# Third attention of a four-layer block: second mask by ScalarE, context projections moved, masks loaded in two steps

## What is computed

```
q = _w8a8_linear(x, wq, bq)          # dynamic 8-bit quantisation of x and wq
k = cond @ wk.T + bk
v = cond @ wv.T + bv
scores = einsum('bhnd,bhld->bhnl', q, k) * inv_sqrt_d + mask[:, None]
attn = softmax(scores, axis=-1)
o = einsum('bhnl,bhld->bhnd', attn, v)
return _w8a8_linear(o, wo, bo)       # quantises o per row, again 8 bits
```

## Time and profile before

| what | value |
|---|---|
| runs, median (lowest to highest) | 1343.7 us (1342.25 to 1351.01), 3 runs |
| profiled execution, its own time | 1340.98 us |
| its span from first to last instruction | 1339.2 us |
| mean granted clock of TensorE over the span, as a share of 2.4 GHz | 0.931 |
| PE busy | 1083.3 us (81%) |
| DVE busy | 853.1 us (64%) |
| ACT busy | 542.5 us (41%) |
| POOL busy | 507.0 us (38%) |

### The profile page before, as it was taken

The page is one execution under the profiler, slowest core; times in us unless marked ns, Lnnn a source line. Parts: engine busy times, 40 slices in busy tenths (PEclk is TensorE's granted clock), DMA queues, the critical chain, the costliest instruction groups (busy, mean ns, idle before and its releaser), DMA issues.

```text
span 1339.2 us, 32909 instructions
## 1 busy us (share of the span) xinstructions
PE 1083.3 (81%) x11717; PEld 832.2 (62%) x11717; DVE 853.1 (64%) x2361; ACT 542.5 (41%) x1049; POOL 507.0 (38%) x1023
## 2 busy tenths in 40 slices
PE   4889898885676588887998799999856569989898
PEld 2566666664575244445666567666644449878798
DVE  2665566565454698975666577777756656555475
ACT  2455454554453477662000132323211644346533
POOL 2444554454884888711001111111313214520261
PEclk8898999898798599998999899999868989989999
DMA  5332223501575455421000000000010630124331
GB/s 181 122 112 69 96 89 127 179 18 36 163 215 178 129 148 145 129 90 64 1 0 0 24 25 16 24 16 23 0 40 4 177 94 32 65 95 152 115 106 64
DMA packets 105784, 112.61 MB, mean 84 GB/s; under 512 B 12548, under 2 KB 95636, under 8 KB 104892
## 3 DMA queue, kind: packets, MB, share of 16 engines
q1 hardware_dynamic: 96732, 88.47, 21.1%
q0 software_dynamic: 8064, 22.06, 5.4%
q10 hardware_dynamic: 864, 0.43, 0.1%
HBM read 66.07 MB, written 44.84 MB: 83 GB/s over the span
## 4 chain that ended last, share of the span: by engine, by line
PE 54%; DVE 17%; issue 10%; ACT 6%; DMA 6%; POOL 3%; SPq 1%; another core or an unknown queue 1%; DVEq 1%; ACTq 0%; POOLq 0%
PE psum L2640 5%; DMA PT<-xs 4%; PE psum L1082 3%; PE psum L2395 2%; DVE mx L852 2%; PE psum L1667 2%; PE psum L1665 2%; ACT ext L2347 2%; PE psum L1666 2%; ACT PT L2338 2%; PE psum L1065 2%; PE psum L1014 2%; PE psum L2380 1%; PE psum L1045 1%; DVE mx L2532 1%
## 5 line engine op out<-in xcount | busy, mean ns | idle before, releaser
L755 POOL TENSOR_SCALAR veps<-mv 128x1 f32<-128x1 f32 x112 | 27.0, 241 | 494.9 <-DVE mv L742 324.8
L852 DVE TENSOR_REDUCE mx<-psum 128x6 f32<-128x960 f32 (+3 forms) x80 | 80.7, 1008 | 77.3 <-PE psum L1050 62.5
L733 POOL DMA_INDIRECT got<-ys,rows_y x64 | 63.9, 999 | 117.9 <-DMA ys<-yt 91.7
L939 ACT ACTIVATE PT<-psum 128x1024 f32<-128x1024 f32 x64 | 65.6, 1025 | 76.6 <-PE psum L1070 76.5
L2298 DVE TENSOR_REDUCE mx<-psum 128x4 f32<-128x1024 f32 x64 | 77.0, 1206 | 19.7 <-PE psum L2369 18.7
L2338 ACT ACTIVATE PT<-psum 128x1024 f32<-128x1024 f32 x64 | 65.5, 1024 | 36.4 <-PE psum L2380 34.7
L1665 PE MATMUL psum<-xnTh,w7h 128*128 128x256 f32 x256 | 76.0, 297 | 1.9 <-issue 1.9
L2640 PE MATMUL psum<-mskp,ident_r 128*128 128x512 f32 x256 | 71.2, 414 | 7.5 <-DVE mx L2532 6.4
L2109 DVE SCALAR_TENSOR_TENSOR x<-psum,cw,x 128x256 f32 (+1 forms) x128 | 53.0, 476 | 36.2 <-PE psum L2057 35.9
L1666 PE MATMUL psum<-xnTl,w7h 128*128 128x256 f32 x256 | 74.0, 289 | 0.6 <-issue 0.6
L1667 PE MATMUL psum<-xnTh,w7l 128*128 128x256 f32 x256 | 73.9, 289 | 0.0
(11 more groups left out here) (412 smaller groups left out, 3425.6 us busy)
## 6 DMA issues: line engine op xcount, KB each, us to landing
xs<-qpad SPq DMA_DIRECT2D x17, 1024.0 KB
PT<-xs SPq DMA_DIRECT2D x78, 128.0 KB, 2.1
ys<-yt SPq DMA_DIRECT2D x78, 128.0 KB, 2.2
ctxT<-in_ctxT SPq DMA_DIRECT2D x48, 128.0 KB
ext<-qscr SPq DMA_DIRECT2D x96, 64.0 KB
w_raw<-in_w SPq DMA_DIRECT2D x16, 384.0 KB, 3.4
arena<-in_w SPq DMA_DIRECT2D x4, 1280.0 KB, 10.0
q_parts<-kscr SPq DMA_DIRECT2D x66, 64.0 KB
```

What stands on the lines that cost most here:

```text
L733: pool.indirect_dma_start(out=dst[:, t % 4, k], out_offset=None, in_=ys[:], in_offset=bass.IndirectOffsetOnAxis(ap=rows_y[:, t, k:k + 1], ...
L852: V.tensor_reduce(mx0[:, u0:u0 + m].rearrange("p j e -> p e j"), src, axis=AX.X, op=ALU.max, negate=True).then_inc(F("mx").sem, 1)
L939: A.activation(PT[:, 1024 * r:1024 * (r + 1)], bank(6, 2), ACT.Exp).then_inc(F("p").sem, 1)
```

## The change

The second mask is no longer laid by matmuls. ScalarE copies the transposed mask (`msk[:, s, 1]`, repeated for eight heads) as plain float32 into two banks at a time, after the reduce of these banks, and TensorE waits for it before the selector matmuls of these banks. POOL splits only the first mask. The V and K projections of the next batch stand between the values of p and the transpose of the maxima; K goes to bank 0 and is copied out before x's transpose is written there. SP loads the context after `k_psum`, the mask after `msk`, the transposed mask after ScalarE's copies.

```diff
@@ s4_sp
+            def load_context(b, s):
                 sp.dma_start(ctxT[:, s], a["ctxT"][:, b]).then_inc(F(f"ctx_loaded{s}").sem, 16)
+            def load_mask(b, s, which):
+                sp.dma_start(msk[:, s, which], a[("mask", "maskT")[which]][:, b]).then_inc(F(f"msk_loaded{s}").sem, 16)
                     sp.wait_ge(F("k_psum").sem, F("k_psum").at(b, 1))
+                    load_context(i * 2 + (u + 2), u)
                     sp.wait_ge(F("msk").sem, F("msk").at(b, 2))
-                    load(i * 2 + (u + 2), u)
+                    load_mask(i * 2 + (u + 2), u, 0)
+                    sp.wait_ge(laid.sem, laid.at(b, 2))
+                    load_mask(i * 2 + (u + 2), u, 1)
@@ s4_pool
-                P.tensor_copy(mskp[:, s, :, 0], msk[:, s]).then_inc(F("msk").sem, 1)
+                P.tensor_copy(mskp[:, s, 0, 0], msk[:, s, 0]).then_inc(F("msk").sem, 1)
                 pool.wait_ge(F("msk").sem, F("msk").at(b, 1))
-                P.tensor_tensor(mskp[:, s, :, 1], msk[:, s], mskp[:, s, :, 0].bitcast(F32), ALU.subtract).then_inc(F("msk").sem, 1)
+                P.tensor_tensor(mskp[:, s, 0, 1], msk[:, s, 0], mskp[:, s, 0, 0].bitcast(F32), ALU.subtract).then_inc(F("msk").sem, 1)
@@ s4_act
             def first():
+                copy_k(0, 0)
                 copy_x(0)
-                copy_k(0, 0)
                 copy_q(0, 0)
+            def lay_mask(b, s, k):
+                wait("mx", b, k + 1)
+                A.copy(bank(4 + 2 * k, 2).rearrange("p (h q) -> p h q", h=8), msk[:, s, 1].unsqueeze(1).to_broadcast([128, 8, T])).then_inc(laid.sem, 1)
             def body(p, b, n, s, turn, turn_b):
                 if p is not None:
                     copy_values(p)
+                for k in range(2):
+                    lay_mask(b, s, k)
+                if n is not None:
+                    copy_k(n, 1 - s)
                 wait("st", b, 1)
                 for k in range(2):
                     A.activation(PT[:, 1024 * k:1024 * (k + 1)], bank(4 + 2 * k, 2), ACT.Exp).then_inc(F("p").sem, 1)
                     if k == 0 and n is not None:
                         copy_x(n)
-                if n is not None:
-                    copy_k(n, 1 - s)
@@ s4_pe
             def transpose_x(b):
                 wait("quant", b, 6)
+                wait("k", b, 2)
-            def project(b, s, turn):
+            def project_context(b, s, turn):
                 wait(f"ctx_loaded{s}", turn, 16)
                 for c in range(2):
                     MM(bank(1)[:, C:2 * C], ctxT[:, s, c], wvT[:, c], start=(c == 0), stop=(c == 1))
+                for g in range(2):
+                    for c in range(2):
+                        t = MM(bank(0)[:, 128 * g:128 * (g + 1)], wkT[:, c, g], ctxT[:, s, c], start=(c == 0), stop=(c == 1))
+                t.then_inc(F("k_psum").sem, 1)
+
+            def project(b):
                 wait("xT", b, 1)
                 for c in range(2):
                     t = MM(bank(1)[:, 0:C], qxT[:, c], qwT[:, 0, c], start=(c == 0), stop=(c == 1))
                 t.then_inc(F("q_psum").sem, 1)
-                for g in range(2):
-                    for c in range(2):
-                        t = MM(bank(2)[:, 128 * g:128 * (g + 1)], wkT[:, c, g], ctxT[:, s, c], start=(c == 0), stop=(c == 1))
-                t.then_inc(F("k_psum").sem, 1)
             def first():
+                project_context(0, 0, 0)
                 transpose_x(0)
-                project(0, 0, 0)
+                project(0)
                 transpose_q(0)
@@ body of s4_pe
                 if p is not None:
                     values(p, 1 - s)
-                for k in range(2):
-                    wait("mx", b, k + 1)
-                    add_mask(s, 1, k)
+                if n is not None:
+                    project_context(n, 1 - s, turn)
                 wait("mparts", b, 4)
...
                 for r in range(4):
+                    if r % 2 == 0:
+                        pe.wait_ge(laid.sem, laid.at(b, r // 2 + 1))
+                        plain(pe)
...
                 if n is not None:
                     transpose_x(n)
-                if n is not None:
-                    project(n, 1 - s, turn)
+                    project(n)
```

More of the change, by code:

```diff
@@ L2431, in s2_pe @@
             s2_turns(body)
+        laid = f[4, "silu"]
         def s4_sp(sp):
             F = lambda n: f[4, n]
-            def load(b, s):
+            def load_context(b, s):
                 sp.dma_start(ctxT[:, s], a["ctxT"][:, b]).then_inc(F(f"ctx_loaded{s}").sem, 16)
-                sp.dma_start(msk[:, s, 0], a["mask"][:, b]).then_inc(F(f"msk_loaded{s}").sem, 16)
-                sp.dma_start(msk[:, s, 1], a["maskT"][:, b]).then_inc(F(f"msk_loaded{s}").sem, 16)
-            load(0, 0)
-            load(1, 1)
+            def load_mask(b, s, which):
+                sp.dma_start(msk[:, s, which], a[("mask", "maskT")[which]][:, b]).then_inc(F(f"msk_loaded{s}").sem, 16)
+            for b in range(2):
+                load_context(b, b)
+                for which in range(2):
+                    load_mask(b, b, which)
             with sp.Fori(0, NB // 2 - 1) as i:
@@ L2681, in body @@
                     wait("p", b, k - 1)
-                    add_mask(s, 0, k)
+                    add_mask(s, k)
                 wait("k", b, 2)
```

8 lines of the change are left out of this document (4 added, 4 removed).

## The result

| what | before | after |
|---|---|---|
| median (lowest to highest), us | 1346.53 (1342.25 to 1351.01), 4 runs | 1360.28 (1355.23 to 1367.21), 4 runs |
| ratio, 95% interval | | 1.0091 (1.0058 to 1.0124) |
| profiled execution, its span, us | 1339.2 | 1365.4 |
| mean granted clock | 0.931 | 0.912 |
| PE busy, us | 1083.3 | 1069.7 |

By the ratio the change costs 0.9%, 12 us, where 6 were forecast (1350 against 1343.7, the median then known). The profiled execution of the changed kernel was the slowest of its four, so its span is no measure of the loss. The changed kernel was timed twice more, each time beside the kernel before on the same chip: 1.0075 (1.0049 to 1.0100) and 1.0071 (1.0042 to 1.0100).

The account below looks back on a forecast made before the run. TensorE was busiest, but the prediction read VectorE as the lap's path, hiding the second mask nearly whole. Terms -3.7 - 0.5 + 0.5 + 11.3 + 0.7 = +8.3 us on 1340.98 gave 1349.3, let stand at 1350; range 1336 to 1363.

Parts of the forecast that it names:

- Second mask off TensorE: Transpose of the maxima starts when VectorE's split is done: 0.23 us gained per lap, -3.7 us (0 to -4.8).
- tempting 35 us: Second mask's whole TensorE busy time, 16 laps of 2.2 us, which the prediction did not expect to gain.
- ScalarE's copies: Two copies of the transposed mask per lap, 1.1 us each, hidden by 0.4 us or more ahead of the selector matmuls.
- Context projections moved: V and K projections fit ahead of the maxima's transpose and were off the path before; gain or loss 0.
- SP, 0: Later, stepwise loads of context and masks cost nothing, being for batches two laps off.
- Start of the stage: Batch 0's projections ahead of x's transpose, at the lower clock: +0.5 us (-1 to +1.5).
- POOL's sums: After the last, halved split, POOL's seven sums for a later stage begin and end earlier: -0.5 us (0 to -1.0).
- the last lap: TensorE waits over 2 us for the split maxima; lower clock then costs +1.5 us at half a chance, +0.7.
- The clock: Emptied place behind the second scores: one in four of 15 laps falls, 3.0 us each, +11.3 us; chance 0.48.
- the covering: A fall slows q's transpose, output projection, first mask and first scores, together +2.8 to +3.3 us if all covered.
- rule of the Trainium skill: VectorE work between matmul groups does not break warmth, long waits do; clock stays, sum -3.7 us; chance 0.26.

Follow-up runs that it names:

- mask alone: Changed kernel, ScalarE still laying the second mask, but V and K projections and the copy of k back at their old places; ratio 1.0094 to the kernel before.
- doubled copy: Changed kernel with ScalarE's first copy of the mask, into the first two banks, made twice; ratio 1.0046 to the kernel before.
- lull alone: Kernel before, TensorE still laying the second mask, with V and K projections of batches 1 to 15 left out; ratio 1.0042 to the kernel before.
- one step: Changed kernel with SP loading context and both masks together behind ScalarE's copies, as in the kernel before; ratio 1.0059 to the kernel before.
- filler: Changed kernel plus matmuls of constants, result unread, where V and K projections used to stand; ratio 0.9982 to the kernel before.
- before with the early half: Kernel before, without the change, with half of the next lap's first mask moved behind its K projection; ratio 0.9948 to the kernel before.
- split: Changed kernel with the V projection at its new place and the K projection with its copy at its old one; ratio 1.0019 to the kernel before.
- output first: Changed kernel, half the next first mask behind the Q projection, also the output projection ahead of q's transpose; ratio 0.9875 to the kernel before.
- early half mask: Changed kernel with half of the next lap's first mask moved behind the Q projection; ratios 0.9871 and, repeated, 0.9903 to the kernel before.

## Why the prediction was right, and which of its sizes were off

The time fell inside the range (1336 to 1363), on its upper side, and the ratio inside 1%, though its interval (1.0058 to 1.0124) reaches over that line. The mechanism forecast as the largest term, the clock falling in some laps of the emptied place, is what happened. That the total came so near is partly luck: terms that were too small and terms that were too large offset each other. The forecast had -3.7 for the mask, -0.5 for POOL, +0.5 at the start, +11.3 for falls and +0.7 for the last lap. The stage shows -5.4 in the laps at full clock, +8.2 for the steady falls, +1.2 for the fall in the first lap, +1.1 ahead of it, +0.9 in the last distance and -0.2 behind it. Added to the median of 1343.7 the forecast's own sum would have been 1352, not the 1350 that was let stand.

**Second mask off TensorE, -0.23 us per lap.** Right at its place: 3.82 us became 3.59, and VectorE has no idle time in the trace before the copy. The tempting 35 us were never there. But only two thirds of the 0.23 arrive, and the mask alone gives 0.15 us per lap. Behind the copy the selector matmuls, which now wait for ScalarE's copies too, start 0.46 us later where it was 0.38 (874.57 to 874.95 before, 829.68 to 830.14 now). The Q projection and q's padded form keep that delay (4.03 us behind the copy for 3.95, and 5.19 for 5.12). So the way from the copy on does not run through VectorE alone, as the prediction had it. That it is the added wait is likely, not tested.

**ScalarE's copies, 1.1 us each, hidden.** 1.02 us, hidden, with about 0.85 us to spare by the doubled copy. Right.

**Context projections moved, 0.** Missed. The step looked at operands only. In the full-clock laps the loop's jump no longer costs its 0.4 us every second lap (13.9 became 13.2 or 13.3). Beside the mask alone the move is worth 0.13 us in a lap without the jump (13.34 to 13.2) and 0.45 in one with it (13.75 to 13.3). The 0.13 stand between q's transpose and the first mask, 0.75 us apart before and in the mask alone, 0.63 in the changed kernel and the lull alone. The prediction had ruled out that anything comes earlier there; yet before, ScalarE's copy of p's output stood behind the copy of k and ended at 880.73, only 0.06 us ahead of the output projection (880.79), and the projection started 0.56 us behind q's transpose, now 0.49. 15 laps of the forecast's 0.23 are 3.5 us; the 14 laps alone gained 5.4.

**SP, 0.** Right, by the kernel that loads in one step.

**Start of the stage, +0.5.** It was +1.1 to the first reduce. There the V projection ran at full clock (1.10 us, not the 2.02 that were assumed), and the first mask took 3.76 us, mostly at the lower one, where it had taken 2.46: the clock came back later in the stage. The first lap is another 1.4 longer (14.49 for 13.06), but that is a fall in its lull, as in the steady laps, and belongs to the term of the clock. Both together pass the upper bound of +1.5.

**POOL's sums, -0.5, and the last lap, +0.7.** Both missed. POOL's sums fall into the last distance of the table, which grew by 0.9 us in place of shrinking: its mean granted clock was 0.66, before 0.82. In the filler kernel the clock stayed at 1.00 there, and the distance was 17.47 us. The fall feared in the last lap itself did not come: TensorE waited 2.40 us for the split maxima, and the selector matmuls behind took 1.06 us, as at full clock. From the last maxima to the stage's end it is 0.2 us less.

**The clock, 3.75 falls of 3.0 us, +11.3.** The mechanism is shown, by the filler that takes the falls away and by the mask alone that moves them. The two sizes were off in opposite ways. There are 5 steady falls in after's profile (4 to 6 in its repetitions and in the kernel that loads in one step), one in three laps, where one in four was taken; with the one in the first lap there are 6 of 15. And a single fall costs 1.2 to 1.3 us, below my lower bound of 1.5; only the neighbouring two, at 16.03 and 14.82 us, cost 4.3 together. The step that failed is the covering: I let a fall hit q's transpose, output, the whole mask and the first scores. In the trace of such a lap (886.50 to 894.50 above) the clock was back before the mask was done (2.80 us in place of 2.11) and the scores ran at full speed (1.17). Together the steady falls cost some 8 us, with the first lap's some 9, against 11.3.

The rule of the Trainium skill that I weighed ("TensorE: Matmul & The Clock Gate", "Loop structure matters more than you think") would have kept the clock here. The trace does not agree: no wait of TensorE in this lull is longer than 1.19 us, and the clock falls.

**The sum.** Forecast +8.3 us; the stage shows +5.6. The three ratios, 1.0091, 1.0075 and 1.0071, stand for 9 to 12 us. So 4 to 7 us lie outside the stage or between executions, where the code is the same. The profiles show where they can be seen: behind the stage TensorE was at 1.2 GHz for 59, 50 and 48 us in the changed kernel's three profiles, and for 44 us in the profiles of the kernel before, of before with the early half and of the loads in one step (worked out from the granted clock in stretches of 20 us). The stages behind took 360.0, 354.0 and 346.8 us in the first three and 347.0, 342.6 and 343.6 in the others. On the first chip the other three kernels had 349.7 to 352.0 beside the changed kernel's 354.0, on the third 342.6 to 344.5 beside 346.8. But the kernel with the loads in one step, with 6 falls in the stage, had none of it, so whether the change causes this stays open. A shifted start of the following stages may change where their clock falls; no run was made to test that.

## What to carry to other kernels

Matmuls taken from TensorE are worth what waits for them, 0.15 to 0.23 us here of 2.2 us busy, and they may have been what held the clock up. Before removing work from an engine, look at which place of the lap becomes empty, and put real work from the path into it in the same edit: here half of the next lap's first mask turned +0.7% into -1%, of which the early half alone, without the change, gives 0.5. To find out whether a loss comes from the clock, matmuls of constants in the empty place are a cheap test.

## What the hardware showed that I had not expected

A fall is short: in a steady lap it costs 1.2 to 1.3 us. Where TensorE idled in one piece (mask alone, 2.40 us) two long falls like the one above cost 4.25 and 4.05 us over two laps each. The wait alone does not decide it: it was 2.39 or 2.40 us in each of laps 2 to 14, and 8 of them kept the full clock (13.33 to 13.78 us).

The loop's jump is not a fixed price. Before, in a lap with the jump and in one without (timeline, output projection and first mask):

```profile
867.25 0.39 PE L2670 MATMUL psum<-qwT,qoT 128*128 128x256 bf16 x2
867.47 2.11 PE L2640 MATMUL psum<-mskp,ident_r 128*128 128x512 f32 x8
...
880.79 0.39 PE L2670 MATMUL psum<-qwT,qoT 128*128 128x256 bf16 x2
881.37 2.10 PE L2640 MATMUL psum<-mskp,ident_r 128*128 128x512 f32 x8 [0.18 <-issue]
```

The mask starts 0.58 us behind the projection with the jump, 0.22 without. With the K projection in the lull the laps alternate by 0.4 us (before, mask alone, split, and before with the early half). Without it they alternate by 0.1 (after, filler, lull alone, one step, output first), and with the early half mask by 0.2. Filler matmuls of K's shape don't bring it back, so it isn't how full TensorE is. SP's loads, which follow K's end and stand up to 2 us ahead of the jump in the kernels that pay, are not enough either: in lull alone they stand there too (the last at 880.13, the mask at 881.26). What it is stays open.
